# An audio tower on one core: a softmax of its own for the first eight pairs, fp32 spreads from row tiles, grams summed by GpSimd, and the order of the roots

## The reference

```
pad time to 752 = 94 windows of 8
scores  = sum over channels of x * w + b                 # one score per batch and step
weights = softmax of the scores inside each window of 8
h       = sum over the window of x * weights             # (128, 94, 64): "tokens"
h += attention(layernorm(h)):
     q, k, v from one linear map; 8 heads of 8 channels
     qgr, kgr = Q factors of the QR decomposition of q and k (94 x 8 per head)
     three score maps: q.k, (q.k)^2, (qgr.kgr)^2, batch-normed, mixed over 24 -> 8 maps,
     softmax, times v, output projection
h += expert FFN(layernorm(h)): one shared and one routed expert per batch pair, two layers
```

## Time and profile before

| | |
|---|---|
| median of three runs | 888.25 us |
| the profiled execution, its own time | 884.84 us |
| its span | 883.0 us |
| busy: PE / DVE / ACT / POOL | 765.8 / 721.0 / 447.0 / 492.6 us |
| mean granted TensorE clock | 0.937 of full |
| DMA | 77.63 MB, mean 88 GB/s |

### The profile page before, as it was taken

How to read it: one execution, slowest core, us unless ns; L and a number is a source line. 1 busy time by engine, 2 the same in 40 slices (tenths; PEclk the granted TensorE clock), 3 DMA queues, 4 the chain that set the end, 5 groups by cost and what they waited for, 6 DMA issues and landing times.

```text
span 883.0 us, 39788 instructions
## 1 busy us (share of the span) xinstructions
PE 765.8 (87%) x16837; PEld 565.1 (64%) x16837; DVE 721.0 (82%) x1408; ACT 447.0 (51%) x927; POOL 492.6 (56%) x532
## 2 busy tenths in 40 slices
PE   4488887666694599999999999999999999899994
PEld 2245444434674478877777778877777887466663
DVE  4388888885579589999999999999999999667772
ACT  2253424321344165565655565665565556477773
POOL 3233333331000578888888888888888887222220
PEclk9789899896697599999999999999999999899998
DMA  8756662662570122222222222222222221001111
GB/s 295 284 168 198 197 197 58 130 128 58 155 143 2 48 76 64 65 64 64 64 66 65 79 65 64 64 64 64 66 73 71 64 64 45 1 22 29 28 29 33
DMA packets 89197, 77.63 MB, mean 88 GB/s; under 512 B 37145, under 2 KB 79708, under 8 KB 89052
## 3 DMA queue, kind: packets, MB, share of 16 engines
q1 hardware_dynamic: 88524, 73.83, 28.9%
q10 hardware_dynamic: 528, 1.54, 0.5%
HBM read 59.23 MB, written 13.04 MB: 82 GB/s over the span
## 4 chain that ended last, share of the span: by engine, by line
PE 51%; DVE 10%; issue 3%; ACT 1%; POOL 0%; POOLq 0%; ACTq 0%; DVEq 0%
PE ps_dot L1116 10%; PE ps_m L1140 8%; PE ps_a L1166 7%; PE ps_a L1158 7%; PE ps_a L1252 4%; DVE row_max_o L1376 3%; DVE row_max_e L1378 3%; PE ps_a L1129 3%; DVE row_max L1364 2%; PE ps_m L1102 2%; PE ps_a L1237 2%; DVE sums L1396 2%; PE ps_dot L1209 1%; PE ps_a L1260 1%; PE ps_dot L1227 1%
## 5 line engine op out<-in xcount | busy, mean ns | idle before, releaser
L1295 ACT ACTIVATE sq<-ps_dot 128x376 f32<-128x376 f32 x384 | 165.0, 482 | 158.4 <-PE ps_dot L1116 150.4
L1116 PE MATMUL ps_dot<-q_st,k_blk 64*64 64x94 f32 x6144 | 170.5, 249 | 1.1 <-ACT sq L1295 0.8
L1116 PEld LDWEIGHTS ps_dot<-q_st,k_blk 64*64 64x64 f32 x6144 | 134.6, 134 | 52.8 <-issue 28.8
L557 POOL TENSOR_TENSOR x_g<-x_g,w_odd 128x752 f32<-128x752 f32 x32 | 57.0, 1780 | 104.4 <-ACT w_odd L493 104.4
L1038 POOL TENSOR_TENSOR v_blk<-v_rep,vmask 128x384 f32<-128x384 f32 x128 | 106.6, 854 | 7.6 <-PE ps_m L1146 5.5
L1053 POOL TENSOR_TENSOR half<-prob 128x564 f32<-128x564 f32 x64 | 75.6, 1181 | 60.7 <-ACT prob L1290 60.7
L1060 POOL TENSOR_TENSOR k_blk<-k_cm,hmask 128x768 f32<-128x768 f32 x64 | 96.7, 1511 | 1.0 <-PE ps_a L1158 1.0
L1062 POOL TENSOR_TENSOR k_mix<-k_cm,cols 128x768 f32<-128x768 f32 x64 | 96.8, 1512 | 0.0
L1364 DVE TENSOR_REDUCE row_max<-ps_a 128x94 f32<-128x564 f32 x128 | 89.4, 740 | 4.5 <-PE ps_a L1166 4.4
L1166 PE MATMUL ps_a<-sq,mix_w 64*32 64x282 f32 x2048 | 81.8, 404 | 0.5 <-ACT sq L1295 0.5
L1140 PE MATMUL ps_m<-prob,v_blk 128*64 128x94 f32 x1536 | 76.6, 248 | 1.1 <-ACT prob L1290 1.1
(11 more groups left out here) (219 smaller groups left out, 1450.7 us busy)
## 6 DMA issues: line engine op xcount, KB each, us to landing
v_rep<-v_rows SPq DMA_DIRECT2D x128, 192.0 KB, 3.1
x_g<-in_x_dram SPq DMA_DIRECT2D x15, 1500.0 KB, 6.5
qk_rows_kept<-tok SPq DMA_DIRECT2D x16, 384.0 KB
qk_rows<-qk_rows_kept SPq DMA_DIRECT2D x4, 1536.0 KB, 11.2
v_rows<-tok SPq DMA_DIRECT2D x16, 192.0 KB
q_st<-q_cm SPq DMA_DIRECT2D x64, 47.0 KB, 1.8
out_dram<-rows SPq DMA_DIRECT2D x16, 188.0 KB
x_g<-in_x_dram ACTq DMA_DIRECT2D x1, 1500.0 KB, 7.1
```

The lines of the kernel that those rows point to most:

```text
L1116: mm = pe.matmul(ps_dot[64 * v:64 * v + 64, (2 * g + b) % 3, N * c:N * c + N], k_blk[rows, a, SLOTS * (3 * v + g) + c].rearrange("p k h m ...
L1295: act.activation(sq[:, b, :, g, :], ps_dot[:, (2 * g + b) % 3, 0:SLOTS * N].rearrange("p (c n) -> p c n", c=SLOTS), ACT.Square).then_inc(s ...
```

## The change

- The first 8 pairs' scores are made once more in a bank of their own, ps_first, in `constants`. Their softmax is made there (ACT and DVE) into the second of now two buffers of `soft`. The first group's full softmax moves into steps 0 and 1 of `pool_project` and serves pairs 8 to 15; `spread` takes the held weights for pairs 0 to 7. The scores made ahead for group 1 go two at a time beside spreads 2 to 9 (AHEAD_FIRST).
- `spread` reads `soft` in fp32: for each half of the 752 columns one matmul of 32 rows (rows 0 to 31, rows 32 to 63) in place of two bf16 matmuls of 128 rows. `parted` and its tiles go.
- ACT copies the grams out of ps_c (`grams_out`), and POOL does what DVE did: mask, then two additions of halves. `centre` waits for ACT's copy. DVE has neither `gram_own` nor `gram_sum`.
- In `orthogonalise` ACT takes the roots ahead of the eighth of the ten expert banks, DVE waits for the top rows only where it first reads them, and `rows` holds the first rows as `aug` does, channel by channel, so that the copy into it reads in the order in which they lie.
- The matmuls of mix_rows come ahead of the last four pairs' scores. The variable EVICT, which chose between two ways of which one was used, goes.

```diff
-def score_pair(pe, x_g, x_in, ps_score, k, a, n, turn):
+def score_pair(pe, x_g, x_in, ps_score, k, a, n, turn, pairs=GP):
...
+            dve.wait_ge(first_out, 1)
+            step(dve.tensor_reduce(first_stat[:, 0, :], soft[:, 1], AX.X, ALU.max))
+            step(dve.tensor_tensor(soft[:, 1], soft[:, 1], over(first_stat[:, 0, :]), ALU.subtract))
+            marks["first_shifted"] = done
...
             marks["mix_rows"] = done
+            dve.wait_ge(first_exps, 1)
+            step(dve.tensor_reduce(first_stat[:, 1, :], soft[:, 1], AX.X, ALU.add))
+            step(dve.reciprocal(first_stat[:, 2, :], first_stat[:, 1, :]))
+            step(dve.tensor_tensor(soft[:, 1], soft[:, 1], over(first_stat[:, 2, :]), ALU.mult))
...
+            act.wait_ge(first_scored, 1)
+            scores = soft[:, 1].rearrange("p w k -> p (w k)")
+            for quarter in range(4):
+                rows = slice(32 * quarter, 32 * quarter + 32)
+                half, at = divmod(quarter, 2)
+                out = act.activation(scores[32 * half:32 * half + 32, at * (TP // 4):(at + 1) * (TP // 4)], ps_first[rows, 0:TP // 4],
+                                     ACT.Identity, bias=k["tok_bias"][rows])
+            out.then_inc(first_out, 1)
+            act.wait_ge(dve_step, marks["first_shifted"])
+            act.activation(soft[:, 1], soft[:, 1], ACT.Exp).then_inc(first_exps, 1)
...
             def spread(g, n):
-                if n == 0:
-                    if g < NG - 1:
-                        pe.wait_ge(s["scores_out"], g + 1)
-                    pe.wait_ge(s["mid_moved"], g + 1)
-                    pe.wait_ge(s["lo_done"], g + 1)
+                if g < NG - 1 and n == (0 if g else 2):
+                    pe.wait_ge(s["scores_out"], g + 1)
+                if n == (0 if g else GP // 2):
+                    pe.wait_ge(s["weights_done"], g + 1)
+                held = 1 if g == 0 and n < GP // 2 else g % 2
                 pe.wait_ge(s["odd_out" if n % 2 else "even_done"], g * HP + n // 2)
                 for half in range(2):
-                    for part in range(2):
-                        mm = pe.matmul(ps_spread[:, 2 * (n % 2) + half, 0:HALF], k["pair_sel"][:, half, n, :], parts[:, g % 2, part, :],
-                                       start=(part == 0), stop=(part == 1))
+                    mine = slice(32 * half, 32 * half + 32)
+                    mm = pe.matmul(ps_spread[:, 2 * (n % 2) + half, 0:HALF], k["pair_sel"][mine, n, :], flat[mine, held, :], start=True, stop=True)
...
             def centre(c):
...
-                    pe.wait_ge(s["gram_owned"], c)
+                    pe.wait_ge(s["gram_out"], c)
...
+            def grams_out(c):
+                act.wait_ge(s["gram_done"], c + 1)
+                if c:
+                    act.wait_ge(s["gram_summed"], c)
+                act.activation(own[:].rearrange("p b g e -> p (b g e)"), ps_c[:, 0:256], ACT.Copy).then_inc(s["gram_out"], 1)
...
+            def gram_sum(c):
+                pool.wait_ge(s["gram_out"], c + 1)
+                pool.tensor_tensor(own[:], own[:], k["mask4"][:].unsqueeze(1).unsqueeze(3).broadcast_to([128, 2 * CP, 4, D]), ALU.mult).then_inc(s["gram_owned"], 1)
+                pool.wait_ge(s["gram_owned"], c + 1)
+                pool.tensor_tensor(own[:, :, 0:2], own[:, :, 0:2], own[:, :, 2:4], ALU.add).then_inc(s["gram_halved"], 1)
+                pool.wait_ge(s["gram_halved"], c + 1)
+                pool.tensor_tensor(gram[:, span(c, 2 * CP), :], own[:, :, 0, :], own[:, :, 1, :], ALU.add).then_inc(s["gram_summed"], 1)
...
             for n, (l, lo, hi) in enumerate(EXPERT_BANKS):
+                if n == ROOTS_AT:
+                    act.wait_ge(dve_step, DIAG_STEP)
+                    act.activation(rs[:], diag[:], ACT.Sqrt).then_inc(roots, 1)
...
-            act.wait_ge(dve_step, DIAG_STEP)
-            act.activation(rs[:], diag[:], ACT.Sqrt).then_inc(roots, 1)
...
-            tt(rows[:], aug[:, :, :, 2 * D:3 * D].rearrange("p k d n -> p k n d"), rs[:].unsqueeze(2).broadcast_to([128, KH, D, D]), ALU.mult)
+            tt(rows[:], aug[:, :, :, 2 * D:3 * D], rs[:].unsqueeze(3).broadcast_to([128, KH, D, D]), ALU.mult)
```

More of the change, by code:

```diff
@@ L50, in score_pair, with constants @@
         mm = pe.matmul(ps_score[32 * quarter:32 * quarter + 32, 0:TP // 4], k["score_w"][:, n, :],
[L51 removed]
+                       x_g[:, a, n, quarter * (TP // 4):(quarter + 1) * (TP // 4)], start=(n == 0), stop=(n == pairs - 1))
     return mm
[L55 removed]
+def constants(nc, p, x_g, x_in, ps_score, soft, k):
     sem = nc.semaphore
@@ L145, in _ @@
             diagonal(k["delta_q"][:], 0, [[-8, 16], [-1, 8]], 1)
-            for quarter in range(4):
-                diagonal(row_sel[32 * quarter:32 * quarter + 32, quarter % 2, :], 0, [[-1, 32]], 1)
+            for half in range(2):
+                diagonal(row_sel[32 * half:32 * half + 32, :], 0, [[-1, 32]], 1)
             marks["pool"] = done
@@ L246, in _ @@
             act.wait_ge(pool_step, marks["pool"])
-            for half in range(2):
-                act.activation(k["pair_sel"][:, half].rearrange("p n (b c) -> p (n b) c", b=2),
-                               row_sel[:, half, :].unsqueeze(2).broadcast_to([128, 32, C]), ACT.Copy)
+            act.activation(k["pair_sel"][:].rearrange("p n (b c) -> p (n b) c", b=2),
+                           row_sel[:].unsqueeze(2).broadcast_to([64, 32, C]), ACT.Copy)
+            act.wait_ge(first_scored, 1)
[8 more added lines that the diff above has]
+            act.activation(soft[:, 1], soft[:, 1], ACT.Exp).then_inc(first_exps, 1)
         @block.tensor
@@ L477, in softmax @@
                         half, at = divmod(quarter, 2)
-                        out = act.activation(flat[32 * half:32 * half + 32, at * (TP // 4):(at + 1) * (TP // 4)], ps_score[rows, 0:TP // 4],
+                        out = act.activation(flat[32 * half:32 * half + 32, g % 2, at * (TP // 4):(at + 1) * (TP // 4)], ps_score[rows, 0:TP // 4],
                                              ACT.Identity, bias=k["tok_bias"][rows])
@@ L529, in _ @@
                     deviation(c)
-                    if EVICT[0] == "act":
-                        scaled(c, 0)
                 if i < STEPS:
                     odd_weights(i)
-                if c is not None and EVICT[1] == "act":
-                    scaled(c, 1)
                 c = chunk_at(i, 3)
@@ L557, in _ @@
                     pool.tensor_tensor(odd, odd, w_odd[:, i % 2, :], ALU.mult).then_inc(s["odd_done"], 1)
-                c = chunk_at(i, 4)
-                for h in range(2):
-                    if c is not None and EVICT[h] == "act":
-                        bias(c, h)
-                if i < STEPS - HP and i % HP == 5:
-                    parted(pool, i // HP + 1, "rest")
-                if i < STEPS - HP and i % HP == 6:
-                    parted(pool, i // HP + 1, "lo")
+                c = chunk_at(i, 5)
+                if c is not None:
+                    gram_sum(c)
         @block.vector
@@ L659, in _ @@
                     softmax(i // HP + 1, i % HP - 4)
-EVICT = ("dve", "dve")
+                if i < 2:
+                    softmax(0, i)
 def span(c, n):
@@ L815, in _ @@
                 for place, product in places:
+                    if j == 0 and product is prods_t:
+                        dve.wait_ge(top_turned, 1)
                     count(dve.tensor_tensor(product[:, :, 0:left, :], fac[:, :, 0:left].unsqueeze(3).broadcast_to([128, KH, left, D]),
```

139 lines of the change are left out of this document (46 added, 93 removed).

## The result

| | before | after |
|---|---|---|
| median of four runs each | 888.87 us | 910.40 us |
| lowest to highest | 887.52 to 890.45 | 907.86 to 913.91 |
| the profiled execution, time / span | 884.84 / 883.0 us | 907.97 / 906.1 us |
| mean granted TensorE clock | 0.937 | 0.883 |
| busy: PE / DVE / ACT / POOL | 765.8 / 721.0 / 447.0 / 492.6 us | 827.8 / 713.7 / 447.5 / 506.7 us |

The ratio is 1.0244, with a 95% interval of 1.0197 to 1.0292. I had forecast 867 us, and a chance of 0.05 for slower. PE got 62 us busier, although a spread now has two matmuls and not four.

A forecast was written before the change was run, and what follows sets the result against it. In the steps neither DVE nor PE is full, so each waits for the other. The terms -6.4 + 0.6 - 2.8 + 0.8 - 7.2 - 5.1 - 1.5 give -21.6, 863.2 us; the median's 3.4 makes 867, range 860 to 873 (0.62).

The forecast's parts named there:

- rival B: In the steps, spreads of fewer active rows leave PE at 1.2 GHz: 911 us, slower than before; chance 0.05.
- chunks with scores: Five chunks of the steps where PE's list decides, and the longer spreads with it: +0.8 us in all.
- softmax chunks: Three chunks of the steps holding the next group's softmax: -2.4 us each, -7.2 in all; -1.1 each at the low clock.
- The spreads: In the steps, two fp32 matmuls side by side take 0.9 us a spread in place of 0.81: +0.08.
- rival A: The two fp32 matmuls of a spread go one behind the other: 882 us, hardly faster; chance 0.08.
- The drain at a change of tiling mode: Between centre and spreads, 0.18 us twice a chunk in 15 chunks would put the sum 5.4 us higher.
- The start: First spread at 26.8 in place of 35.14, product 2 at 36.7 in place of 43.12: -6.4 us.
- rival D: DVE's savings become waits in all chunks: 878 us; chance, with its like, 0.14.
- The grams: Taken from DVE in the steps: -2.8 us in chunks without scores, -7.2 in those with a softmax.
- Orthogonalise: DVE's wait for the roots shrinks, -5.1 us, and head_rows takes 1.2 in place of 2.71, -1.5.
- Attend: The attention and the FFN, where no line changes, keep their 586.8 us.
- Rival C: PE stays at full speed in the steps, and start and softmax chunks reach their ends: 855 us; chance 0.09.

The follow-up runs named there:

- e4: The kernel before with its bf16 spreads over rows 0 to 63 alone, the middle part of the weights left out: 917.27 us, ratio 1.0347.
- e6: e1 with the first eight pairs' softmax among the constants, spreads still bf16 over 128 rows: 870.97 us, ratio 0.9804.
- e1: The kernel before with the grams on ACT and POOL and the orthogonalise edits, its spreads and start unchanged: 872.83 us, ratio 0.9845.
- e3: The kernel before with fp32 spreads, one matmul of 128 rows for each half, padded with zeros: 889.43 us, ratio 1.0033.
- e8: As e3, with spreads of 64 rows in place of 128: 942.29 us, ratio 1.0616.
- e5: The changed kernel with its fp32 spreads padded with zeros to 128 rows: 876.78 us, ratio 0.9873.
- e11: The kernel before with bf16 spreads from two 32-row tiles, the middle part of the weights left out: 903.22 us, ratio 1.0209.

## Why the prediction was wrong, point by point

- **The clock: rival B, and the step that failed.** I gave B 0.05 with the words "PE's busy time in columns stays, and its longest pauses get shorter". Both are so, and neither holds the clock: the rows of 180 to 220 us have PE busy for 99% at 0.50. B had the mechanism (fewer active rows leave PE at 1.2 GHz, and PE's list becomes the bound) and the time, 911 against 910.4. That the two times agree so closely is luck: B put 5.5 us on each of eight chunks with scores and nothing on the others; the trace has the low clock in chunks without scores too, 13.5 us for one against 10.4 before. The step that failed is that the sum has no term for the clock, since its chance was put at 0.05. The runs show what stands in its place: +31.0 us in the steps from before to e4, whose spreads differ from each other in nothing but rows, and +31.15 from product 2 to orthogonalise in the changed kernel, for which the sum had -8.6.
- **The clock in the terms.** I priced chunks by full-clock waits, also the softmax chunks, whose -2.4 each supposes that PE runs at full speed behind the softmax; its clock went lower instead. The granted clock of 0.86 in the earlier trace rows should have been read as a warning: the stage already had stretches at 1.2 GHz.
- **The spreads** were right for what they were: 0.90 us at full clock, side by side, and rival A is refuted. At 1.2 GHz it is 1.62. The drain at a change of tiling mode, which the Trainium skill names ("TensorEngine Tiling", Key Properties), shows in this trace, in the starts and not in the lengths. Before, centre and the spread behind it overlap by 0.16 us (127.99 + 0.91 - 128.74); in the changed kernel, where the spread is in tiles, by 0.07 (140.95 + 0.91 - 141.79). So a change costs 0.09 us at the full clock, half of my estimate of 0.18, and small beside the term of the clock. The rows of before:

```profile
127.99 0.91 PE L398 MATMUL ps_c<-tokens,cent_w 128*128 128x384 f32 x2
128.74 0.80 PE L386 MATMUL ps_spread<-parts,pair_sel 128*128 128x376 bf16 x4
```

- **The start** was 3.65 us and not 6.4 earlier at product 2. The first spread came 1.1 us after my 26.8, and I let PE answer at once, while spread and scores at the low clock (3.1 us a pair) were what product 2 waited for. Worse, I took all of it as time of the kernel: of e6's gain of 8.5 us at the first spread 1.7 were left at the end of the steps. What rival D had for the whole change, a gain that turns to waits, happens to this term.
- **The grams** were right in mechanism: ACT's copy takes 0.38 us, POOL 0.61 + 0.46 + 0.32, and PE stands 1.0 us for it in all 16 chunks together. They are worth 6.6 us in the steps (e1), where my chunks had -2.8 - 7.2, with +0.8 for the spreads.
- **Orthogonalise** was right: -6.9 for -6.6. The roots still cost a wait of 1.12 us (I had said under 0.6), and head_rows takes 1.22 for 2.71.
- **Attend**, counted as untouched, pays 2.5 us. In its first 20 us PE is granted 0.72 where before it had 0.78; whether that is all of it isn't shown. In e1 attend is 2.4 us shorter than before, and nothing of it is edited there either, so it varies by as much untouched.
- **Rival C's sum** doesn't come out of its pieces: three times 2, 1.9 for the start and three times 0.35 from 866.6 give 857.6, not 855. Nothing else rests on it.

## What to carry to other kernels

A matmul that uses fewer rows of the array can take no longer itself and still cost the clock of everything around it. Before taking rows away from a frequent matmul in a stage that doesn't sit at 2.4 GHz all the time, price the whole stage at 1.2 GHz and give that case real weight, and if it comes true, padding with zeros to 128 rows may give the faster kernel even where the matmul takes 1.7 times as long (1.53 against 0.90 us here). And a block that starts 8 us earlier has won only what is still there at the stage's last event.

## What the runs showed of the hardware that I had not expected

- The granted clock isn't a matter of pauses alone. PE busy for 19.8 of 20.0 us had 1.2 GHz; in the same stage of before, busy for 13.3 of 20.0 us, it had 2.4 GHz. The Trainium skill ("TensorE: Matmul & The Clock Gate", Part 1) puts the clock down to how busy TensorE has lately been; with busy time as the profile counts it, this trace disagrees. Rows aren't all of it either: e3 and the kernel before both have spreads of 128 rows, of 1.53 us in fp32 and of 0.81 in bf16, and clocks of 0.94 and 0.86; whether the length or the type makes that difference isn't shown.
- Rows of zeros count. e8 lacks nothing of e3 but rows 64 to 127, whose data are zeros, and has a clock of 0.72 over the steps for 0.94. e3 and e5 have the highest clock of all.
- A change between the whole array and tiles of it has a price of 0.09 us at the full clock, which shows in the next start: the overlap of centre with the spread behind it falls from 0.16 to 0.07 us. The same 0.07 stands in e8 and in e11, whose spreads are in tiles of 64 and 32 rows, and the same 0.16 in e3, whose spreads have 128, so it isn't the type.
- The response is uneven: one 128 x 128 filler per spread left the clock at 0.64, two raised it to 0.80; half of the spreads with 128 rows gave 0.88, none 0.63, all 0.94.
- bf16 matmuls in two row tiles take 0.49 us a spread where one behind the other they take 0.80; in fp32 0.90 and 1.53.
